# A gather ring of six groups in place of five in the key loops of a graph network kernel, laid over other buffers

## The reference

```python
for l in range(L):                                   # L = 2
    xn = _layernorm(h, ln1_g[l], ln1_b[l])
    q = (xn @ wq[l] + bq[l]).reshape(n, H, DH)       # H = 8 heads of 32
    k = (xn @ wk[l] + bk[l]).reshape(n, H, DH)
    v = (xn @ wv[l] + bv[l]).reshape(n, H, DH)
    scores = jnp.einsum('ehd,ehd->eh', q[dst], k[src]) * scale
    m = jax.ops.segment_max(scores, dst, num_segments=n)
    ex = jnp.exp(scores - m[dst])
    z = jax.ops.segment_sum(ex, dst, num_segments=n)
    agg = jax.ops.segment_sum((ex / z[dst])[:, :, None] * v[src], dst, num_segments=n)
    ...                                              # output projection, feed-forward
```

## Time and profile before

| | us |
|---|---|
| runs of the kernel before: median (lowest, highest), 3 runs | 5205.84 (5201.02, 5213.5) |
| the profiled execution | 5207.07 |
| its span, first to last instruction | 5205.9 |

### The profile page before, as it was taken

How to read it: one execution, slowest core, us unless ns; L and a number is a source line. 1 busy time by engine, 2 the same in 40 slices (tenths; PEclk the granted TensorE clock), 3 DMA queues, 4 the chain that set the end, 5 groups by cost and what they waited for, 6 DMA issues and landing times.

```text
span 5205.9 us, 59946 instructions
## 1 busy us (share of the span) xinstructions
PE 3587.0 (69%) x15291; PEld 2665.8 (51%) x15291; DVE 2874.2 (55%) x6726; ACT 1846.5 (35%) x5462; POOL 3690.2 (71%) x3085
## 2 busy tenths in 40 slices
PE   4554444466897444439979946666589999688886
PEld 3433323344575232326646634444368887577776
DVE  6465556888543454568884336677752224244445
ACT  1143333566333343337753311111120100256565
POOL 4466666888888666678888876666787887866664
PEclk9866676899898667669999868777799999789988
DMA  7688888565324888866653245566569899556565
GB/s 262 195 278 285 270 288 245 130 159 130 55 25 110 273 272 284 276 183 177 169 138 34 14 91 171 172 173 175 100 153 269 240 267 253 152 174 175 174 175 141
DMA packets 710880, 951.03 MB, mean 183 GB/s; under 512 B 273285, under 2 KB 482228, under 8 KB 710408
## 3 DMA queue, kind: packets, MB, share of 16 engines
q0 software_dynamic: 298192, 385.84, 31.0%
q1 hardware_dynamic: 204146, 388.26, 23.7%
q10 hardware_dynamic: 208198, 173.03, 10.1%
HBM read 727.03 MB, written 219.80 MB: 182 GB/s over the span
## 4 chain that ended last, share of the span: by engine, by line
PE 28%; issue 24%; DVE 15%; POOL 15%; another core or an unknown queue 9%; DMA 6%; ACT 2%; DVEq 1%; ACTq 1%; POOLq 0%; SPq 0%
PE bank L2677 10%; POOL ATT L981 7%; POOL sc L967 7%; PE bank L2802 6%; PE bank L2799 4%; DVE arena L1485 3%; DMA sc<-arena 2%; PE bank L2382 2%; PE bank L2517 2%; DMA ATT<-arena 2%; DVE arena L1395 2%; DVE arena L1765 2%; PE bank L2658 1%; DVE arena L1466 1%
## 5 line engine op out<-in xcount | busy, mean ns | idle before, releaser
L944 POOL DMA_INDIRECT arena<-KVT,arena x832 | 800.7, 962 | 484.5 <-issue 268.4
L2517 PE MATMUL bank<-arena 128*128 128x264 f32 x1664 | 599.0, 514 | 674.5 <-issue 332.2
L2517 PEld LDWEIGHTS bank<-arena 128*128 128x128 f32 x1664 | 390.9, 251 | 881.9 <-issue 588.3
L997 POOL DMA_INDIRECT arena<-ATTR,arena x416 | 666.8, 1603 | 152.2 <-issue 152.2
L967 POOL DMA_INDIRECT sc<-arena x391 | 641.4, 1640 | 130.4 <-issue 110.9
L981 POOL DMA_INDIRECT ATT<-arena x391 | 643.1, 1645 | 125.6 <-issue 114.0
L1485 DVE TENSOR_TENSOR arena<-arena,bank 128x256 f32<-128x256 f32 x832 | 297.4, 412 | 579.8 <-remote 426.8
L944 POOL DMA_INDIRECT arena<-X1T,arena x416 | 413.2, 993 | 245.9 <-issue 134.9
L944 POOL DMA_INDIRECT arena<-YT,arena x416 | 407.4, 979 | 218.5 <-issue 106.5
L2474 PE MATMUL bank<-arena 128*128 128x273 f32 x1664 | 455.0, 411 | 141.3 <-DVE arena L1544 91.7
L2290 ACT ACTIVATE arena<-arena 128x128 f32<-128x128 f32 x1248 | 374.8, 387 | 275.9 <-DVE arena L1371 160.8
(11 more groups left out here) (334 smaller groups left out, 6434.5 us busy)
## 6 DMA issues: line engine op xcount, KB each, us to landing
VE<-arena ACTq DMA_DIRECT2D x208, 512.0 KB
arena<-VE SPq DMA_DIRECT2D x208, 512.0 KB
left<-ATT SPq DMA_DIRECT2D x250, 320.0 KB
left<-AM SPq DMA_DIRECT2D x250, 320.0 KB
ATT<-arena POOLq DMA_DIRECT2D x25, 1600.0 KB, 6.5
arena<-LOCT SPq DMA_DIRECT2D x156, 256.0 KB
arena<-ATT SPq DMA_DIRECT2D x75, 384.0 KB
AM<-arena ACTq DMA_DIRECT2D x75, 384.0 KB
```

Of the source, the lines that this page charges most:

```text
L944: GP.indirect_dma_start(out=ring[:, i % n, k, :], out_offset=None, in_=table, in_offset=bass.IndirectOffsetOnAxis(ap=idx[:, 4 * i + k:4 * ...
L997: GP.indirect_dma_start(out=PA[:, c, 2:6], out_offset=None, in_=ATTR, in_offset=bass.IndirectOffsetOnAxis(ap=PA[:, c, 0:1].bitcast(I), axi ...
L2517: mm = P.matmul(b_[:, 0:264], OHQ[:, i % 3, k * 128:(k + 1) * 128], QS[:, i % 4, k, :], start=True, stop=True)
```

## The change

The ring KV of the key loops has six places in place of five. It then reaches 2048 words further, over the value loop's buffers and into the one-hot buffers up to o_oh + 1304. What lay there moves or shrinks:

- The places of the key loops go to rings of their own over the accumulator (KPLACES, KPLACES2), of two pairs in place of three. Pair j is issued once the one-hot of group 2j-3 is made (before: 2j-5).
- QS has three groups in place of four, and ACT makes group i+2 in step i in place of i+3.
- POOL waits in layer 0 for sw_out(4), the places written out to HBM, ahead of its first gather, as the sixth place lies over LT.
- `tstart`, `wfl`, `kw` and ROWS get other offsets; the semaphores `kept` are six, and what counts on them follows.

```diff
-GATHERS = {"k0": 5, "k1": 5, "l1": 6, "l3": 5}
+GATHERS = {"k0": 6, "k1": 6, "l1": 6, "l3": 5}
...
-    KV = view(o_big, 5, 4, 512)
+    KV = view(o_big, 6, 4, 512)
...
-    QS = view(o_acc + 1536, 4, 4, 264)
-    assert 1536 + 4 * 1056 <= 5800
+    QS = view(o_acc + 1536, 3, 4, 264)
+    KPLACES = view(o_acc + 4704, 4, 256).bitcast(BF)
+    KPLACES2 = view(o_acc + 4704, 2, 512).bitcast(BF)
...
             def load_places(j):
-                if j >= 3:
-                    SY.wait_ge(*onehot(f"k{l}", 2 * j - 4))
-                SY.dma_start(PLACES2[:, j % 3, :], LOCT2[j:j + 1, :].to_broadcast([128, 1024])).then_inc(group_in.sem(j), 16)
+                if j >= 2:
+                    SY.wait_ge(*onehot(f"k{l}", 2 * j - 2))
+                SY.dma_start(KPLACES2[:, j % 2, :], LOCT2[j:j + 1, :].to_broadcast([128, 1024])).then_inc(group_in.sem(j), 16)
...
-            for j in range(3):
+            for j in range(G // 2):
                 load_places(j)
-            for i in range(G):
-                if i % 2 and i + 5 < G:
-                    load_places((i + 5) // 2)
...
+            if l == 0:
+                GP.wait_ge(*sw_out(4))
             for i in range(G):
-                if i >= 5:
-                    GP.wait_ge(*scored(k_, i - 4))
-                    GP.wait_ge(*kept[i % 5](l * len(range(i % 5, G, 5)) + i // 5))
+                if i >= 6:
+                    GP.wait_ge(*scored(k_, i - 5))
+                    GP.wait_ge(*kept[i % 6](l * len(range(i % 6, G, 6)) + i // 6))
                 gather(k_, i, KVT, 512, isrc, o_big)
...
             def stage(i):
                 ws = windows_of(S, regs, wd_i, i)
-                if i >= 4:
-                    S.wait_ge(*q_edge(name, 2 * (i - 3)))
+                if i >= 3:
+                    S.wait_ge(*q_edge(name, 2 * (i - 2)))
                 for k in range(4):
-                    ins = S.activation(QS[:, i % 4, k, :], Q[:, bass.ds(ws[k], 1), :], ACT.Copy)
+                    ins = S.activation(QS[:, i % 3, k, :], Q[:, bass.ds(ws[k], 1), :], ACT.Copy)
                 ins.then_inc(placed.sem, 1)
-            for i in range(3):
+            for i in range(2):
                 stage(i)
             for i in range(G):
-                if i + 3 < G:
-                    stage(i + 3)
+                if i + 2 < G:
+                    stage(i + 2)
```

More of the change, by code:

```diff
@@ L206, in program @@
     bank = [nc.alloc_psum_tensor(f"bank{i}", [128, 512], F) for i in range(8)]
-    tstart = view(o_oht, T)
+    tstart = view(o_oh + 1488, T)
     OHB = view(o_acc, 25, C)
@@ L237, in program @@
     starts = view(o_oh + 560, 2)
-    kw = view(o_w + 1056 + 5 * 2048 + 100, C)
+    kw = view(o_oh + 1912, C)
+    assert o_oh + 1912 + C <= o_sm
     of_bucket, rank, posw = (view(o_acc + 5800 + 400 * k, C) for k in range(3))
@@ L260, in program @@
     o_big = o_w + 1056
-    KV = view(o_big, 5, 4, 512)
+    KV = view(o_big, 6, 4, 512)
     VR = view(o_big, VRING, 4, 256)
-    assert o_big + 5 * 2048 <= o_oh and o_big + VRING * 1024 <= o_wv
+    assert o_big + 6 * 2048 <= o_oh + 1488 and o_big + VRING * 1024 <= o_wv
     BIG = view(o_big, 6400)
@@ L283, in program @@
     OHQ = view(o_acc, 3, 512)
-    QS = view(o_acc + 1536, 4, 4, 264)
-    assert 1536 + 4 * 1056 <= 5800
+    QS = view(o_acc + 1536, 3, 4, 264)
+    KPLACES = view(o_acc + 4704, 4, 256).bitcast(BF)
+    KPLACES2 = view(o_acc + 4704, 2, 512).bitcast(BF)
+    assert 1536 + 3 * 1056 <= 4704 and 4704 + 2 * 512 <= 5800
     D8 = view(o_S, SB, 16, 8)
@@ L306, in program @@
     HT = view(o_S + 2048, 8, 512)
-    ROWS = view(o_oh + 400, 2, 768)
+    ROWS = view(o_oh + 376, 2, 768)
     XXR = view(o_q + 4224, 2, 4, 256)
@@ L487, in program @@
     ordered = [Landed(nc, f"ordered{k}") for k in range(KS)]
-    kept = [Landed(nc, f"kept{k}") for k in range(5)]
+    kept = [Landed(nc, f"kept{k}") for k in range(6)]
     def am_kept(n):
         k = n % AMRING
-        return kept[k](2 * len(range(k, G, 5)) + n // AMRING + 1)
+        return kept[k](2 * len(range(k, G, 6)) + n // AMRING + 1)
     group_in = Slots(nc, VRING, dict(k0=G // 2, v0=G, k1=G // 2, v1=G, l1=G // 2))
@@ L667, in sync_engine @@
                     SY.wait_ge(*tables_out[par](2 * len(range(par, W, 2))))
-            for j in range(3):
+            for j in range(G // 2):
                 load_places(j)
-            for i in range(G):
-                if i % 2 and i + 5 < G:
-                    load_places((i + 5) // 2)
             SY.wait_ge(*scored(f"k{l}", G))
-            for k in range(5):
-                SY.wait_ge(*kept[k]((l + 1) * len(range(k, G, 5))))
+            for k in range(6):
+                SY.wait_ge(*kept[k]((l + 1) * len(range(k, G, 6))))
             def load_emb(n):
@@ L1332, in load_and_project @@
                     finish(w - 1)
-        wfl = view(o_oht, T)
+        wfl = view(o_oh + 1488, T)
         d.mark(V.memset(wrap, 0.0))
@@ L1465, in k_onehot @@
                     V.wait_ge(*q_edge(name, 2 * (i - 2)))
-                V.tensor_scalar(OHQ[:, i % 3, :], PLACES[:, i % 6, :], pcol, None, ALU.is_equal).then_inc(onehot.sem, 1)
+                V.tensor_scalar(OHQ[:, i % 3, :], KPLACES[:, i % 4, :], pcol, None, ALU.is_equal).then_inc(onehot.sem, 1)
             if l == 1:
@@ L1479, in vector_engine @@
             for i in range(G):
-                rows = KV[:, i % 5, :, 0:256]
+                rows = KV[:, i % 6, :, 0:256]
                 V.wait_ge(*gathered(name, i))
@@ L2078, in stage @@
                 ws = windows_of(S, regs, wd_i, i)
-                if i >= 4:
-                    S.wait_ge(*q_edge(name, 2 * (i - 3)))
+                if i >= 3:
+                    S.wait_ge(*q_edge(name, 2 * (i - 2)))
                 for k in range(4):
-                    ins = S.activation(QS[:, i % 4, k, :], Q[:, bass.ds(ws[k], 1), :], ACT.Copy)
+                    ins = S.activation(QS[:, i % 3, k, :], Q[:, bass.ds(ws[k], 1), :], ACT.Copy)
                 ins.then_inc(placed.sem, 1)
-            for i in range(3):
+            for i in range(2):
                 stage(i)
             for i in range(G):
-                if i + 3 < G:
-                    stage(i + 3)
+                if i + 2 < G:
+                    stage(i + 2)
                 S.wait_ge(*gathered(name, i))
-                S.dma_start(VE[i], KV[:, i % 5, :, 256:512]).then_inc(kept[i % 5].sem, 16)
+                S.dma_start(VE[i], KV[:, i % 6, :, 256:512]).then_inc(kept[i % 6].sem, 16)
                 for k in range(4):
@@ L2094, in scalar_engine @@
                                  ACT.Identity, bias=FL[:, 4 * i + k:4 * i + k + 1]).then_inc(self_edge.sem, 1)
-            for k in range(5):
-                S.wait_ge(*kept[k]((l + 1) * len(range(k, G, 5))))
+            for k in range(6):
+                S.wait_ge(*kept[k]((l + 1) * len(range(k, G, 6))))
             copy_scan(f"w{l}", SPs)
@@ L2516, in tensor_engine @@
                         P.wait_ge(*self_edge(name, 4 * i + k - 7))
-                    mm = P.matmul(b_[:, 0:264], OHQ[:, i % 3, k * 128:(k + 1) * 128], QS[:, i % 4, k, :],
+                    mm = P.matmul(b_[:, 0:264], OHQ[:, i % 3, k * 128:(k + 1) * 128], QS[:, i % 3, k, :],
                                   start=True, stop=True)
```

## The result

The changed kernel took 5213.68 us (median of 20 runs, 5197.51 to 5225.91), the kernel before, beside it, 5201.36 (20 runs, 5195.1 to 5218.26). The ratio is 1.0018, 95% interval 1.001 to 1.0027: 9 us more by the ratio, inside the 0.2% that I had called no change, and near its edge. The profiled execution of the changed kernel took 5203.8 us, 10 less than its median, so its stages can't be held against the earlier trace rows by a few microseconds. Lines behind the change have moved by two or so: L1485 is now L1487, L1488 L1490, L1466 L1468, L2090 L2092, L2093 L2095, L2517 L2519, L967 L969, and SP's L659 L662.

What follows compares the result with a forecast made beforehand. Key loops bound by DVE, held by late PE signals under full DMA, so POOL stops every six groups. 5207.1 + 9.7 − 1.0 − 1.0 − 2.0 = 5212.8; against the runs' median 5211.5, called 5211; range 5176 to 5226.

Steps and rivals of the forecast that it cites:

- The gate on sw_out(4): POOL's new wait ahead of k0's first gather: start 9.7 us later, 0 to +9.7 on the path, taken as +9.7.
- a late start isn't made up: Start of k0: POOL's lateness stays on the path, since k0 and k1 both took POOL 630 us despite different head starts.
- The ring, 5 to 6: Key loops: the sixth place buys nothing in steady state, only moves each loop's first wait; −1.0 us a loop, twice.
- The cycle of six groups: Key loops: POOL's wait of 5.9 us falls after the same six groups with six places as with five.
- the 33 to 35 and 175 to 185: Key loops: expected number of POOL's waits on L1488 and their total in us, still, after the change.
- my 628 to 631: Expected length in us of each of the two key loops after the change.
- The end of k0: POOL's 10.15 us wait for L1099 before the scatters shifts with the cycle's phase: −9.9 to +5.0, taken as −2.
- Places and scaled queries: Key loops: place loads issued three groups ahead and queries made one group later cost 0.
- DVE is held while the DMA engines are full, and they empty only once POOL stops: Key loops: PE's signals reach DVE late under full DMA traffic, some 17 and 20 us for group 59.
- the floor of 5.3 us a group: Key loops: 1.70 MB a group at 322 GB/s makes DMA the floor, above POOL's 5.0 us.
- That it is PE's signals: Key loops: DVE's waits ahead of its products are for PE's late q_edge, not for gathered rows.
- P: Theory made after experiment 4, for the key loops: PE's signals arrive late while POOL issues gathers back to back, whatever DMA carries.

Runs made afterwards that it cites:

- Experiment 2: Kernel before, five places kept, with only POOL's early wait on sw_out(4) added: 5185.75 us, ratio 1.0026.
- experiment 1: Changed kernel with POOL's new wait moved from its first gather to group 5, the first using the sixth place: 5174.39 us, ratio 1.0005.
- experiment 3: Kernel before with a gather ring of four places in place of five: 5173.12 us, ratio 1.0000.
- 5: Kernel before, but PE signals q_edge once a group in place of twice and DVE waits once: 5222.55 us, ratio 1.0026.
- experiment 4: Kernel before, but values written to HBM only for the first four groups of each key loop: 5167.77 us, single run.
- experiment 8: Kernel before, but from the fifth group on gathers bring 1 KB a row and no values are written: 5194.11 us, single run.
- experiment 7: Kernel before, but in the key loops SP's plain loads of the same bytes replace POOL's gathers: 4843.91 us, single run.
- 6: Kernel before with a gather ring of two places in place of five: 5431.3 us, ratio 1.0429.
- experiment 9: Kernel before without the key loops' matmuls, DVE reading queries from SBUF and waiting for no PE signal: 4851.02 us, single run, third set's chip.
- 10: Kernel before, ring of five, but POOL issues group i only once group i-2 is scored: 5033.83 us, ratio 1.0459, third set's chip.
- experiment 11: Kernel before, ring of five, but POOL issues group i only once group i-3 is scored: 4817.97 us, ratio 1.0015, third set's chip.
- 12: Kernel before with a gather ring of three places in place of five: 4903.47 us, ratio 1.0182, third set's chip.

## Why the prediction was right where it was, and wrong where it was

**The sign, the size.** Forecast +5.7 us, 5211; measured +9 us by the ratio (12.3 between the medians), 5213.68. The class (within 0.2%) and the range hold.

**The gate on sw_out(4): right, mis-sized a little.** The term was +9.7, nothing absorbed. POOL started 11.3 us later and not 9.7, as it passes the gate 0.86 us after SP does (267.81 and 266.95) and SP passed it 0.8 later than before. Experiment 2 prices the gate alone at +13 us, experiment 1 takes it off the start and is left with nothing. That a late start isn't made up, which I had read from k0 and k1 taking the same 630 us, was the step that carried the sum.

**The ring, 5 to 6: right in its number.** I had it at −1.0 a loop. Six against five with a late gate is +0.05% (−0.05 to +0.15), four against five 0.00% (−0.09 to +0.10): 0 within 5 to 8 us. The cycle of six groups and 36.3 us is seen again with six places. The first stop of k0 came behind nine groups, near the ten I had named; the waits, 32 of 172.5 us, are just under the 33 to 35 and 175 to 185. The loops of the profiled run, 625.7 and 622.1 us, missed my 628 to 631. As about these lengths come with four and five places too (experiments 3 and 2), nothing speaks for the sixth having made them.

**The end of k0: no value to be had.** I had put −2 from bounds of −9.9 and +5.0. In the profile after, the wait of 10.15 us is down to 0.30, as in the best case; yet the medians of 20 runs don't show that gain. The same wait was 0.31 us in experiment 3, 1.09 in 5, 5.68 in 2, 6.14 in 1, 7.84 in 4 and 13.50 in 8, so one execution doesn't give its sign; 0 with wider bounds would have been the better entry. With it and without the −1.0 twice, the sum is +9.7, close to the 9 measured. So the forecast of +5.7 stood on one term that was right and on −4.0 of terms that no run bears out; that they were small is why the number held.

**Places and scaled queries: right, 0.** DVE's one-hots waited 10.8 us in 2 waits for the places, 3.67 of it at the start, none in mid-loop:

```profile
L1468 DVE TENSOR_SCALAR arena<-arena x208: 476/478/703, 270.2 to 2296.5; 128x512 f32<-128x512 bf16 x104
its engine sat idle before it (us, times) until:
  DMA arena<-LOCT: 10.8, 2
```

**The mechanism behind the cycle: wrong.** The step that failed is "DVE is held while the DMA engines are full, and they empty only once POOL stops". The signals were late, but the cause wasn't this. When POOL stops, two things end, the traffic and POOL's issuing, and I named the first. Even the order of events didn't quite bear it: the wait that ended at 639.25 ended while POOL issued its last gather and the DMA engines were still at 0.6 to 0.9, and the one at 628.54 in the midst of full traffic; only the third ended in the silence. Experiments 4 and 8 took traffic away (DMA share 0.67 and 0.41) and the waits stayed; 7 filled the engines and took POOL away, and they went; 6 let POOL pause in every group, and they went. And the floor of 5.3 us a group by 322 GB/s was mis-sized: plain loads moved 396 GB/s. The Trainium skill, "DMA: Bandwidth & Descriptors", section "Specifications", puts HBM's share of a core at some 358 GB/s; the run doesn't agree with it as a cap, as it moved 396 over 300 us on this one core.

The weight on the forecast was still right, since it rested on what is seen (rows had landed and lay), not on why. The two theories differ elsewhere: had the change been one that thins the traffic, I would have promised a gain that experiment 4 shows not to be there.

**That it is PE's signals: shown by the semaphore's own record.** From the earlier trace rows it was only argued that DVE waited for PE's signals; the run that was to show it, experiment 9, met a chip without the effect. The trace of the kernel before settles it, as it also keeps moments at which a semaphore was raised (the rows shown so far only name what ended a wait). Behind the passes of group 59, which began at 621.12, `q_edge` rose at 628.52, 639.15 and 643.40, and then at 643.46, 643.52 and 643.58: four signals, of three groups, 0.06 us apart. DVE's three waits of that cycle ended at 628.54, 639.25 and 643.43. Over both key loops, 75 of the 94 waits of over 2 us ahead of a product ended within 0.25 us of such a rise, and DVE then went on 17 us (median) after the modelled end of the pass it needed; in the changed kernel it was 62 of 86, and 20 us. In experiments 6, 7, 10, 11 and 12 one such wait in each ended so, 0.11 us after the pass.

The other signals of the loop were prompt in the same cycle (kernel before):

```profile
639.70 0.60 ACT L2093 ACTIVATE arena<-bank,arena 128x8 f32<-128x8 f32 x2 [8.43 <-issue]
644.21 1.22 DVE L1488 TENSOR_REDUCE arena<-arena 128x32 f32<-128x1024 f32 x1
```

ACT's copy at 639.70 began 0.03 us after the end of the product that it copies behind (639.25 + 0.42), though its wait is called "issue"; over both loops its 106 waits of over 1 us ended at most 0.17 us after that product. POOL went on at 645.70, 0.27 us after the end of the sum (644.21 + 1.22). So DVE handed on at once, and PE's signal to DVE was the late one. Nor does PE's clock explain it: the four passes from 624.85 took 1.13 us at a granted clock of 1.0 (2.4 GHz), the four from 629.32 took 2.13 us at 0.5 (1.2 GHz); that is one microsecond against 17.

**What stays open.** P is true as far as it was tried on the first chip, and not of the third set's: there POOL issued without a pause at an even higher share of traffic, and nothing was late. So POOL's issuing is at most one of two conditions, and the other goes with the chip or with that set of runs; one chip of either kind can't tell. Where signals are late the trace also lacks many semaphore events: of the 832 products' signals in the key loops it has 301 in the kernel before and 320 in experiment 4, but all 832 in experiment 7 on the first chip and in experiment 11 on the other. That is why "remote" and "issue" name so many waits here. The waits of ACT for the product's signal show it, in the changed kernel and then in experiment 11, where no event is missing (line, instruction, busy us, mean ns, idle us before it, and what ended most of it):

```profile
L2095 ACT ACTIVATE arena<-bank,arena 128x8 f32<-128x8 f32 x832 | 210.5, 265 | 656.9 <-issue 477.0
```

```profile
L2094 ACT ACTIVATE arena<-bank,arena 128x8 f32<-128x8 f32 x832 | 201.8, 265 | 402.8 <-DVE arena L1486 379.2
```

Whether the lost events and the late signals have one cause, and whether the recording itself has a part in it, no run here tells; nor do rows show whether the passes were drawn out behind their recorded start or their signals alone came late. What delays them isn't settled. No kernel here beats the kernel before by more than its interval, apart from those that leave out part of the work.

## What to carry to other kernels

Before a ring is made longer, look whether its rows had landed when the consumer was still waiting: here they lay there, and more places brought nothing, though the producer's waits named the ring. A new wait ahead of the first instruction of the engine that leads the chain counted in full here; put it where the resource is first needed, as experiment 1 did at no measurable cost. When two things stop at the same moment, a trace can't tell which of them was the cause; one run that takes away each can, and both should be on the chip that shows the effect, with the unchanged kernel beside them.

## What the runs showed of the hardware that I had not expected

- The same kernel took 5173 and 5208 us in two sets and 4812 on another chip, 7 to 8% apart. Between the changed kernel and experiment 11 the difference lies in the four loops in which POOL gathers for PE and DVE; the scatters in between took 761.7 us (L967, kernel before) and 765.5 (L968, experiment 11).
- On one chip, `q_edge`'s rises came some 17 us behind the passes, four of them 0.06 us apart, while signals from DVE to ACT and to POOL took 0.03 to 0.27 us in the same cycle.
- A gather of 128 rows cost POOL 0.95 us at 1 KB a row (experiment 8) and at 2 KB. Sent as plain loads, the same bytes took 4.2 us a group (440.6 us of k1 in experiment 7, from the end of one line's scatters at 1481.5 to the start of the next line's at 1922.1, over 104).
- In experiment 9 the gathers were slower for POOL, 1004 ns in the mean against 970 in experiment 11; times 832 that is 28 us, as much as lies between the two spans. It is the kernel in which DVE reads both operands from SBUF. That this is the cause was not tried.
